# Moving one spread of B, B's row transposes, a gate projection and the backward time steps forward in the queues of an attention, Mamba and mixture-of-experts kernel

## The reference

```
x = x + attention(group_norm(x))     # q, k, v by 128x128 weights; each row keeps its 102 largest of 1024 scores, softmax, times v
t = tokens of x                      # (1024, 128)
t = t + core(ln(t)):                 # core adds its own input, and two Mamba blocks, one forward, one backward in time
      xn = ln(input)*gamma + beta
      xs, z = xn @ in_proj.T         # 256 channels each
      xs = silu(causal_conv4(xs))
      dt_in, B, C = xs @ x_proj.T    # 16, 16 and 16 rows
      dt = softplus(dt_in @ dt_proj.T + bias)
      for each of the 16 states s:   h_s(t) = exp(dt*A_s) * h_s(t-1) + (dt*xs) * B_s(t)
      y = sum_s h_s * C_s + xs*D;    y = y * silu(z);   out = y @ out_proj.T
t = t + moe(ln(t))                   # router softmax, best 2 of 8 experts, each gelu(t@w1+b1)@w2+b2
```

## Time and profile before

| | |
|---|---|
| median of 3 runs | 1602.65 us (1600.6 to 1603.63) |
| profiled execution | 1604.47 us, its span 1602.7 us |
| TensorE busy | 1252.0 us, 78% |
| VectorE busy | 1249.7 us, 78% |
| ScalarE busy | 891.2 us, 56% |
| GpSimd busy | 797.2 us, 50% |
| granted TensorE clock over the span | 0.89 of 2.4 GHz |

### The profile page before, as it was taken

One profiled execution on the slowest core, in us unless ns is written; L12 is line 12 of the kernel. 1 busy time (PEld: TensorE's weight loads), 2 busy tenths in 40 slices (PEclk: granted clock), 3 DMA queues, 4 the chain that ended last, 5 costly groups with the idle time before them and its releaser, 6 DMA issues. The chain is left out here.

```text
span 1602.7 us, 17247 instructions
## 1 busy us (share of the span) xinstructions
PE 1252.0 (78%) x4450; PEld 649.7 (41%) x4450; DVE 1249.7 (78%) x1425; ACT 891.2 (56%) x1246; POOL 797.2 (50%) x431
## 2 busy tenths in 40 slices
PE   3428598889867778889984859898986787988867
PEld 1225254334526244334443525433452634443343
DVE  2786679998696669999678668999869576999930
ACT  1726456575645646667483646657564564756713
POOL 2022168786160138878243216878626104877834
PEclk8759689999987869999997958999997876999989
DMA  2000012221120012222020001222102001222203
GB/s 72 13 1 3 28 66 92 79 93 65 41 79 14 4 42 90 103 81 92 15 102 31 3 28 66 92 79 103 54 28 79 14 21 35 92 92 79 96 10 119
DMA packets 30495, 91.90 MB, mean 57 GB/s; under 512 B 4790, under 2 KB 8764, under 8 KB 30428
## 3 DMA queue, kind: packets, MB, share of 16 engines
q1 hardware_dynamic: 30428, 91.10, 16.3%
HBM read 88.34 MB, written 2.75 MB: 57 GB/s over the span
## 5 line engine op out<-in xcount | busy, mean ns | idle before, releaser
L621 POOL TENSOR_TENSOR work<-expo,ring 128x1024 f32<-128x1024 f32 x128 | 300.0, 2365 | 127.7 <-DVE expo L1289 123.6
L621 POOL TENSOR_TENSOR ring<-ring 128x1024 f32<-128x1024 f32 x128 | 300.0, 2367 | 47.0 <-DVE ring L1289 47.0
L1289 DVE TENSOR_TENSOR_SCAN expo<-ring,ps 128x1024 f32<-128x1024 f32 x128 | 286.0, 2270 | 0.0
L1289 DVE TENSOR_TENSOR_SCAN ring<-ring,ps 128x1024 f32<-128x1024 f32 x128 | 284.1, 2261 | 0.0
L1738 PE MATMUL ps<-ring,ident 128*128 128x512 f32 x512 | 262.3, 617 | 27.3 <-POOL ring L621 20.7
L1738 PE MATMUL ps<-work,ident 128*128 128x512 f32 x512 | 240.8, 592 | 0.0
L870 ACT ACTIVATE ring<-dt_f,decay 128x1024 f32<-128x1024 f32 x128 | 146.9, 1151 | 106.1 <-DVE expo L1289 61.3
L668 ACT ACTIVATE b_dtx_tok<-dtx_tok,b_tok 128x256 f32<-128x256 f32 x448 | 189.2, 493 | 0.0
L1701 PE MATMUL ps<-ident,b_dtx_tok 128*128 128x128 f32 x896 | 122.2, 279 | 47.5 <-DVE expo L1289 43.3
L1701 PEld LDWEIGHTS ps<-ident,b_dtx_tok 128*128 128x128 f32 x896 | 96.2, 141 | 139.9 <-DVE expo L1289 70.2
L1738 PEld LDWEIGHTS ps<-ring,ident 128*128 128x128 f32 x512 | 82.9, 189 | 164.9 <-POOL ring L621 126.7
(11 more groups left out here) (258 smaller groups left out, 2088.1 us busy)
## 6 DMA issues: line engine op xcount, KB each, us to landing
ring<-c_rows SPq DMA_DIRECT2D x128, 512.0 KB, 3.5
b_dtx_tok<-comb_rows SPq DMA_DIRECT2D x32, 512.0 KB, 3.6
x_c<-in_x SPq DMA_DIRECT2D x4, 512.0 KB, 3.4
out<-xs_f SPq DMA_DIRECT2D x4, 512.0 KB, 2.6
w<-in_L_ffn_w SPq DMA_DIRECT2D x2, 512.0 KB
ring<-in_L_attn_f_in_proj_w SPq DMA_DIRECT2D x1, 256.0 KB
ring<-in_L_attn_b_in_proj_w SPq DMA_DIRECT2D x1, 256.0 KB
c_rows<-dbc_f SPq DMA_DIRECT2D x4, 64.0 KB, 1.9
```

The costliest lines, as they stand in the source:

```text
L621: pool.tensor_tensor(hc[odd][:, k, :], hs[odd][:, k, :], c_all[:, odd, :], ALU.mult).then_inc(hc_ready, 1)
L1289: v.tensor_tensor_scan(hs[odd][:, k, order], dA[:, k, order], dbu[:, order], 0.0, ALU.mult, ALU.add).then_inc(scan_ready, 1)
```

## The change

The same values are computed, and every tile keeps its place. What changes:

- TensorE: the spread of state 1 goes ahead of `token_major` for the forward direction too. B's rows are brought to tokens by 16 transposes of the 16 rows (`tr`, with a 16x16 identity) where 16 float32 matmuls over all 128 rows with 16 columns of the identity stood. The gate projection of backward block 0 goes ahead of the forward dt projections, and the first backward dt projection ahead of the first spread.
- ScalarE: `b_and_c` is split in two, and the backward float32 copy goes between the two forward logarithms. The backward middle part goes behind the backward logarithms.
- VectorE: the cap of backward block 0 goes ahead of the second forward time step; the backward `rest` behind the first backward time step; the backward `last_part` behind the second.

```diff
@@ ScalarE: b_and_c, prepare, direction @@
                 act.wait_ge(dbc_filled, b * DIRS + d + 1)
                 copy(dbc[d], dbc_ps[d][:, :]).then_inc(hi_ready, 1)
+
+            def parts(b, d):
+
                 copy(bc_parts[d][:, :], dbc_ps[d][0:PARTS * BC, :]).then_inc(hi_ready, 1)
...
                 b_and_c(b, 0)
+                parts(b, 0)
...
                 dt_log(b, 0, 0)
+                b_and_c(b, 1)
                 dt_log(b, 0, 1)
-                b_and_c(b, 1)
+                parts(b, 1)
...
                 if d == 0:
-                    middle_part(b, 1)
                     dt_log(b, 1, 0)
                     dt_log(b, 1, 1)
+                    middle_part(b, 1)
                     act.wait_ge(tok_filled, 5 * b + 1)
@@ VectorE: mamba @@
                 dtx_forward(b, 0)
+                cap_step(b, 1, 0)
                 time_step(b, 0, 1)
                 dtx_forward(b, 1)
                 products(b, 0, 0, 0, 0, first=True)
-                rest(b, 1)
-                cap_step(b, 1, 0)
                 cap_step(b, 1, 1)
                 scan_product(b, 0, 0, 0, 0, 0, 0, first=True)
-                last_part(b, 1)
                 time_step(b, 1, 0)
+                rest(b, 1)
                 scan_product(b, 0, 0, 0, 0, 0, 1, first=True)
                 time_step(b, 1, 1)
+                last_part(b, 1)
                 second_state(b, 0)
@@ TensorE: token_major, first_states, mamba @@
                     pe.wait_ge(dt_ready, b * DIRS * BLOCKS + 4)
+                    passed(pe)
                     for e in range(DIRS):
                         for i in range(TILES):
                             at = (e * TILES + i) * D_STATE
-                            last = mm(ps45[:, at:at + D_STATE], dbc[e][:, i * P:(i + 1) * P], ident[:, 0:D_STATE],
-                                      start=True, stop=True)
+                            last = tr(ps45[:, at:at + D_STATE], dbc[e][0:D_STATE, i * P:(i + 1) * P],
+                                      ident[0:D_STATE, 0:D_STATE])
...
             def first_states(b, d):
-                if d == 0:
-                    token_major(b, d)
                 spread(b, d, 1, 1 - d)
-                if d == 1:
-                    token_major(b, d)
+                token_major(b, d)
                 skip_terms(b, d)
...
                 project_dbc(b, 0, 1)
+                project_z(b, 1, 0)
                 project_dt(b, 0, 0)
                 project_dt(b, 0, 1)
-                project_z(b, 1, 0)
                 project_z(b, 1, 1)
                 project_dbc(b, 1, 0)
                 project_dbc(b, 1, 1)
+                project_dt(b, 1, 0)
 
                 pe.wait_ge(parts_ready, b * DIRS + 1)
                 pe.wait_ge(mid_ready, b * DIRS + 1)
                 pe.wait_ge(dt_ready, b * DIRS * BLOCKS + 2)
                 spread(b, 0, 0, 0, first=True)
-                project_dt(b, 1, 0)
                 project_dt(b, 1, 1)
                 first_states(b, 0)
```

## The result

The changed kernel takes 1552.58 us (median of four runs, 1549.17 to 1554.83) against 1602.06 us (four runs, 1600.6 to 1603.63): ratio 0.9689, interval 0.9668 to 0.9711.

The account below looks back on a forecast made before the run. VectorE was taken to idle 11.2 us per image because of TensorE's queue order. The three steps put the first pair at 207.4 instead of 216.12: 8.7 us, over four images 34.9 off 1602.65, so 1568 us; range 1554 to 1586.

Parts of the forecast that it names:

- step 3: From the last time step to the first pair of states: 14.6 us instead of 18.2.
- Step 1: Up to the start of VectorE's first products: at 180.2, half a microsecond before the old 180.69.
- the quick start: Rival, chance 0.08: gate projection first, projections end up to 3.7 us sooner; gain 10.9 us per image, 1559 us.
- The cap in front: Rival, chance 0.09: waiting for the backward dt projection costs more than earlier gates bring; gain 25 us, 1578 us.
- Step 2: From the first products to the end of the last time step: 12.6 us, ending at 192.8 against 197.94.
- The last part: VectorE's 1.9 us behind the last time step: costs nothing while TensorE's token-major work takes longer.
- Late clock: Rival, chance 0.15: transposes do not raise TensorE's clock, skip terms and sum run at half; gain 21 us, 1582 us.
- Slower: Rival, chance 0.04: TensorE stays at 1.2 GHz into the loop over pairs; two such pairs give 1629 us.
- The signs named in advance: Spread wait under 15 us, 11.2 us idle split in two, last time step 5 us and first pair 8 to 9 earlier.

Follow-up runs that it names:

- e1: Kernel before with one edit: the forward spread of state 1 ahead of the token-major work; 1595.12 us, ratio 0.9966.
- e12: Kernel before with one edit: B's rows by 16 transposes instead of 16 matmuls, in the old order; 1581.18 us, ratio 0.9883.
- e5: Kernel before with three TensorE edits: spread ahead, B's rows by transposes, gate projection first; VectorE's and ScalarE's orders and backward dt projections as before; 1560.44 us.
- e3: Changed kernel with B's rows by 16 matmuls again instead of 16 transposes; 1569.25 us, ratio 0.9798.
- e7: Changed kernel with VectorE's backward last part behind the scans of state 1 and ScalarE's two decays of state 1 ahead of the token-major copies; 1550.29 us.
- e11: As e10, with VectorE's rest between first products and second cap, and last part between first scan and first backward time step; 1549.52 us.
- e2: Changed kernel with the forward spread of state 1 behind the token-major work again; 1559.30 us, ratio 0.9744.
- e10: As e7, and in addition the forward spread of state 2 ahead of the skip terms on TensorE; 1549.06 us, ratio 0.967.

## Why the prediction was right or wrong

The path was right: VectorE's stand behind the token-major work was the place, TensorE's chain to the next spread came last behind it, and the shift of the first pair came through to the end once per image. That shift, 12.4 us, times four is 49.6 us, and the medians say 49.5; that they agree so closely is luck, for over the kernels of the table the two differ by up to 4. Wrong were sizes, above all in step 3, and one reading of the clock. And "the wait is one of order in TensorE's queue" is the smaller part of the truth: the spread's place alone brought 5.9 us (e1), the transposes alone 19.4 (e12).

- **Step 1** was forecast 0.5 us earlier and came 1.4. The table load came 1.7 us earlier in the forecast, 3.0 to 4.9 in the trace. The failing sentence is that the four projections "fill 158.97 to 169.65 in either order": they took 7.4 to 9.0 us for 10.5. Their own rows showed a mixed clock, and the prediction kept this case as the quick start, at 0.08. The cap in front took back 2.3 us (e5 against the changed kernel). That is within the 1.6 to 3.4 of the prediction's own sum, but more than its 180.2 allows, which lies below the 180.6 to 182.4 of that sum. Its best end has no working either: 180.6 less the 3.8 us of quicker projections is 176.8, and not 178.0.
- **Step 2** was forecast 12.6 us and took 12.86 in every image of every kernel with this order. The wait at the second cap was 1.16 us, where 0.6 were forecast and 2.13 stood before.
- **Step 3** was forecast 14.6 us and took 11.8. This is the step that failed, at two terms, both changed by the transposes that replaced the matmuls. "I take 3.4, the row beside it" for the 16 transposes: they take 1.8, below even the 2.2 that the row of the setup gave. The load durations could not have settled it: at the full clock, the trace of before has 136 ns for a load of 8 rows, and for loads of 128 rows 183 in the setup and 140 in the backward transposes. The changed kernel has both forms at the half clock, 0.112 us from one transpose to the next against 0.216; they differ in the rows loaded and in the columns moved (16 against 128), and no run takes the two apart. And "I let them run 3.6 us at the half clock", since the clock had risen 10.5 us after the restart before: with transposes in place of the matmuls it rises after 4.6 to 7.9. I had read the 10.5 us as a time from the restart; the 36 places counted under e3 show it as one from the `dtx` transposes, which the 6.8 us of matmuls had put off. The first term is 1.6 us per image; the skip terms, forecast at 5.3 us, took 4.7 in the first image and 3.6 in the second, where the clock was full, 4.0 in the mean, so the other is 1.3. In all step 3 shrank by 6.65 us where 3.6 were forecast. That is 12 us of the 14.6 by which the forecast missed; step 1 adds 3.5, and step 2 takes 1 back.
- **The last part** was costed at nothing since it ran beside the token-major work. That was right but close: it took 4.0 us instead of 1.9, and e7 shows that moving it away frees nothing while TensorE's chain ends last. In the changed kernel VectorE was done 0.5 to 1.5 us before TensorE in three images, and last in the fourth.
- **Late clock**, the rival at 0.15, is refuted. The Trainium skill, "TensorE: Matmul & The Clock Gate", Part 4, says that the full clock does not engage in transposes; the trace disagrees for the float32 transposes here: at 562.7 it rose after 4.7 us of idle and 5.3 us of nothing but transposes, and in the fourth image at 1293.14, 4.8 us after the restart, while they were still running (to 1293.39):

```profile
1288.36:1293.14 4.78, 4.78 (x30) 4.74 (x31) 4.71 (x3) 1.29 (x2) 4.78 (x2) 0.50 0.01 3
1293.14:1293.40 0.26, 0.26 (x5) 0.26 (x3) 0.26 (x1) 0.23 (x2) 0.26 (x1) 1.00 0.00 0
```

- **The cap in front** did cost 2.3 us, but the quicker projections paid for it. **The quick start** came true in half: the four projections took 7.4 us in two images and 9.0 in the other two. **Slower** did not come near: the pairs run at the full clock as before.
- The signs named in advance came true in part: the wait for the spread is 2.6 us (under 15), the last time step 5.8 us earlier and the first pair 12.4. The 3 us of idle before the second state's scan did not appear, because the decay came sooner, B's rows being 1.6 us shorter than forecast, and the last part ran 2.1 us longer.

The two profiled executions differ by some 6 us more than four times 12.4. The excess lies outside the three steps (the first convolution of the first image is 2.05 us early already), and it is the distance of the two executions from their medians, 2.4 and 3.4 us. What makes executions of one kernel differ so is open.

## What to carry to other kernels

A wait that the profile puts on one instruction tells where the engine stands, not what the edit is worth: with only that instruction moved, 34 of 46 us of waiting passed to the next late one. Price all the chains that end near the same moment first, and look for the term that they share; here it was 16 small float32 matmuls, replaced by transposes at 0.112 us each. And where a clock rises some time after TensorE's restart, look in several images and kernels which instruction the rise follows before moving that delay along as a constant.

## What the runs showed of the hardware

- A transpose of 16 rows with 16 columns out took 0.112 us at the half clock, a float32 matmul of 128 rows with 16 columns 0.426 (two instructions of 0.213), a transpose of 128 columns 0.216, each from one start to the next.
- VectorE's subtraction of two SBUF tiles of 32x1024 took 1.22 us alone (before, e11) and 3.26 beside GpSimd's multiplication of two SBUF tiles (changed, e2, e7, e10); GpSimd's own took up to 3.26 instead of 2.35 beside VectorE's. VectorE's products and scans, which read PSUM, kept their 1.23 and 2.28 us beside the same GpSimd work. It was not so each time: `rest`, also a subtraction of two SBUF tiles, began 0.2 us ahead of GpSimd's multiplication in the changed kernel and kept its 1.21 us, while the multiplication took 3.2 instead of 2.34. What they share was not tried apart.
